# Own rows and projected rows turned by transposing DMAs in place of TensorE, in a two-layer, two-block graph network

## The chip, the cores and the metric
One core of one Trainium2 chip. The metric is the device time of one launch in microseconds (us), inputs and output in DRAM.

## The reference
x has 3125 nodes of 128 features; src and dst name 50,000 edges, sorted by dst. Two blocks follow each other; each adds a two-layer graph network of the normalised, rectified x to x.

```python
h = maximum(layernorm(x), 0)
# block 1: agg(h) = segment_sum(h[src], dst) * inv_deg
h1 = relu(concat([h, agg(h)]) @ W1 + b1)             # 128+128 -> 256
x  = x + log_softmax(concat([h1, agg(h1)]) @ W2 + b2)  # -> 128
h = maximum(layernorm(x), 0)
# block 2: mean(h) = segment_sum(h[src], dst) / max(deg, 1)
h3 = relu(mean(h)  @ W_l0.T + b_l0 + h  @ W_r0.T)    # -> 256
h4 = relu(mean(h3) @ W_l1.T + b_l1 + h3 @ W_r1.T)    # -> 256
out = x + relu(h4 @ W_lin1.T + b_lin1) @ W_lin2.T + b_lin2
```

## The kernel before
**Layout.** The nodes are cut into 25 tiles of 125 rows (P = 125) and seven chunks of columns: six full ones of 500 nodes (C, four tiles) and one of 125. Activations are kept in two ways: by rows, each node's values as an f16 high half and an f16 low half side by side (`hs_a`, `hs_b`, 125 partitions, per tile 2 x 128 columns), and turned, features on the partitions and nodes along the free side (`aggT`, `actT`, `zT`, `selfT`).

**Aggregation.** The edges are made into a dense matrix of edge counts, `adj`, in SBUF. `aggregate` (L1036) multiplies, for one chunk, every tile's high and low half by the 500 columns of `adj`: 50 matmuls per chunk and phase, accumulated in a bank of PSUM. `adj` is itself built by matmul: for each group DVE compares keys with a ramp (`group`, L493 for full chunks, L497 for the last), PE multiplies the one-hots (`count`, L990), and ACT copies the result out (L844). There are four buffers for one-hots, of which three go round, so DVE runs at most three groups ahead of PE.

**Phases.** Phase 1 aggregates the rows in `hs_a` and computes h1 and, because aggregation and projection commute, already projects: self = h1 times the own half of W2 (kept, stored to `self_d`), and z = h1 times the other half, scaled by a power of two, turned back to rows and written to `hs_b` as high and low halves. Phase 2 aggregates z, adds self, takes log_softmax, adds x (to `x1_d`), normalises, and writes the new rows to `hs_a`. Phase 3 aggregates them and makes h3; phase 4 aggregates h3 and ends with the two linear layers.

**Order within a chunk.** Each engine runs a program written out by hand; a step of chunk c also finishes chunk c-1. In phase 1 a step of PE (`step1`, L1112) is: own rows of chunk c-1 (`own1`, L1066: eight f16 matmuls by an identity, L1046, into bank 6); the first count and aggregate; six more; `hidden1` (eight f32 matmuls, L1053); six pieces; `second1` (eight more, for z and self); twelve pieces; `turn1` (L1086: four transposes of zT, L1090, into bank 3). Counts for chunk c+1 are woven between the aggregates of chunk c. The same step of DVE (L635): one group; `agg_out` (L615, scaling by the inverse degrees; it waits for their load); three groups; `low` of chunk c-2 (L626, low half of z); groups 4 to 18; `self_out` (L621); groups 19 to 24. ACT (L883): `h0_turned` (L856, bank 6 to aggT); `high` (L876); the evictions of the counts, with `relu` (L863) and `z_out` (L871) between. The first chunk (`first1`) has no predecessor; step 1 (`second=True`) also computes the bounds for the power-of-two scales and turns the weights.

Phases 2 to 4 share `staged` (L1176): chunk 0 is aggregated first, with the last parts of the phase before at set tiles (`lead`), then each step runs its `parts` at set tiles. Phase 3's parts are `own3` (L1250) at tile 0, `turn3` at 0, `hidden3` (L1254) at tile 8; ACT copies bank 3 to aggT (L957). At tiles 20 and 24 of chunk 0 PE waits for the last rows of the phase before (`source`).

**Queues.** All loads and stores of the layers are issued by SP, in one program and one queue. In phase 1 it stores the inverse degrees (L276), waits for them, loads those of chunk 0 (L291), and then per chunk waits for `p1_agg_out`, loads the next inverse degrees, waits for `p1_self` and stores self (L321); in step 0 it also stores the turned weights (L272), for which it waits. In phase 2 it loads inverse degrees, self and x, and stores x1 (L351). In phase 3 it loads inverse degrees and stores h3. A general path (`slow`) for graphs that do not fit the buffers is in the same program; a flag computed from the data picks one.

```python
def wait_past(eng, name, value):
    if not isinstance(value, int) or value > 0:
        eng.wait_ge(sem(name), value)
```

## Time and profile before

| | |
|---|---|
| median of 3 runs (lowest, highest) | 588.14 us (587.84, 588.85) |
| the profiled execution's own time | 587.56 us |
| its span, first to last instruction | 585.7 us |
| mean granted TensorE clock | 0.992 |
| PE busy | 544.2 us, 3078 matmuls |
| DVE, ACT, POOL busy | 225.0, 202.9, 24.7 us |
| own-row matmuls (L1046), all phases | 100, eight to a full chunk |
| DMA traffic | 29.47 MB, mean 50 GB/s |

Busy is the time in which an engine executes something; the span is 1.86 us shorter than the time. "Idle before, releaser" names what an engine waited for. The chain is the sequence of work that ended last, followed back from the end; its starts and durations follow the completion of each piece and so differ by some tenths from the timeline's. L numbers are lines of the kernel. DMA share is the mean busy share of 16 DMA engines. The phases lie at about 48 to 203 us (phase 1), 203 to 282 (phase 2), 282 to 380 (phase 3) and from there on (phase 4); building the first part of `adj` and normalising x fill the time before 48.

### The profile page before, as it was taken

The page shows a single profiled execution, that of the slowest core. Times are in us where ns is not written, and L with a number is a line of the kernel's source. Part 1 is how long each engine was busy: PE and PEld are TensorE (multiplying, and loading weights), DVE is VectorE, ACT ScalarE, POOL GpSimd, SP SyncE. Part 2 cuts the span into 40 slices and gives each one's busy share as a digit, 9 for nine tenths or more (in the row PEclk, how much of TensorE's full clock was granted, in tenths as well). Part 3 has the DMA queues.
Part 4 walks back from the last instruction along what each step waited for, and adds up shares of the span by engine and source line. Part 5 has one row for each costly group of instructions (what it writes and reads, how often), then busy time and mean ns, then how long its engine had stood idle before and what let it go on. Part 6 is the DMA issues. An engine that isn't in the chain of part 4 may idle for free.

```text
span 585.7 us, 9420 instructions
## 1 busy us (share of the span) xinstructions
PE 544.2 (93%) x3078; PEld 291.5 (50%) x3078; DVE 225.0 (38%) x500; ACT 202.9 (35%) x368; POOL 24.7 (4%) x36
## 2 busy tenths in 40 slices
PE   1367999999999999999999999999999999999996
PEld 0244655555554654445455555644545445454555
DVE  6899959577775217667411111110000001010001
ACT  1688858567664304455422222200000010100011
POOL 4410000000000000110100000000000000000000
PEclk9997999999999999999999999999999999999999
DMA  3800103010010124333121111232011212111011
GB/s 94 196 1 1 38 1 117 2 36 17 17 35 17 24 70 112 90 90 77 39 76 53 52 52 39 67 117 52 19 35 39 49 35 52 35 35 52 17 32 30
DMA packets 31372, 29.47 MB, mean 50 GB/s; under 512 B 4894, under 2 KB 30879, under 8 KB 31215
## 3 DMA queue, kind: packets, MB, share of 16 engines
q1 hardware_dynamic: 29622, 27.91, 17.6%
q10 hardware_dynamic: 1561, 0.84, 0.6%
q0 software_dynamic: 160, 0.33, 0.2%
q8 instruction: 18, 0.29, 0.2%
q14 instruction: 11, 0.09, 0.0%
HBM read 19.68 MB, written 9.39 MB: 50 GB/s over the span
## 4 chain that ended last, share of the span: by engine, by line
PE 87%; DVE 5%; ACT 3%; DMA 2%; issue 2%; POOL 1%; ACTq 0%; SPq 0%; DVEq 0%; POOLq 0%
PE ps L1036 54%; PE ps L1053 22%; PE ps L990 6%; PE ps L1308 2%; DVE hs_b L493 2%; PE ps L1046 1%; PE ps L1270 1%; DMA hs_b<-self_d 1%; DMA adj<-key_d,adj 1%; ACT adj L1490 1%; POOL adj L1375 1%; PE ps L1242 1%; DVE adj L1426 1%; DMA adj<-in_dst_dram 0%; ACT adj L844 0%
## 5 line engine op out<-in xcount | busy, mean ns | idle before, releaser
L1036 PE MATMUL ps<-adj,hs_b 125*128 (+2 forms) x1050 | 203.6, 351 | 0.0
L1036 PE MATMUL ps<-adj,hs_a 125*128 (+2 forms) x700 | 158.5, 353 | 0.0
L1036 PEld LDWEIGHTS ps<-adj,hs_b 125*128 125x128 f16 x1050 | 96.3, 97 | 103.9 <-issue 6.6
L493 DVE TENSOR_TENSOR hs_b<-iota,hs_b 128x1024 f16<-128x1024 f16 x150 | 95.4, 685 | 27.9 <-PE ps L990 26.9
L844 ACT ACTIVATE adj<-ps 125x500 f32 (+2 forms) x150 | 80.0, 544 | 22.8 <-PE ps L990 16.6
L990 PE MATMUL ps<-hs_b 128*128 128x125 f16 x625 | 68.5, 233 | 20.7 <-DVE hs_b L493 13.1
L990 PEld LDWEIGHTS ps<-hs_b 128*128 128x128 f16 x625 | 46.5, 103 | 65.7 <-DVE hs_b L493 34.4
L1036 PEld LDWEIGHTS ps<-adj,hs_a 125*128 125x128 f16 x700 | 58.5, 98 | 38.8 <-issue 5.4
L975 ACT ACTIVATE actT<-ps,col 128x500 f32<-128x500 f32 (+1 forms) x14 | 8.9, 633 | 148.0 <-PE ps L1053 148.0
L791 DVE TENSOR_TENSOR hs_a<-ps,hs_a 125x512 f32<-125x512 f32 (+1 forms) x7 | 4.4, 634 | 128.9 <-PE ps L1308 128.9
L1053 PE MATMUL ps<-aggT,wts 128*128 128x500 f32 (+1 forms) x112 | 44.6, 540 | 0.4 <-ACT aggT L957 0.4
L759 DVE TENSOR_TENSOR aggT<-ps,invc 128x500 f32<-128x500 f32 (+1 forms) x7 | 4.4, 622 | 64.9 <-PE ps L1036 61.6
L1053 PEld LDWEIGHTS ps<-aggT,wts 128*128 128x128 f32 x112 | 19.8, 190 | 18.8 <-issue 17.2
L782 DVE TENSOR_TENSOR aggT<-ps,invc 128x500 f32<-128x500 f32 (+1 forms) x14 | 8.7, 619 | 50.1 <-PE ps L1036 44.9
L1053 PE MATMUL ps<-wts,hs_a 128*128 128x500 f32 (+1 forms) x56 | 23.5, 541 | 0.6 <-DVE aggT L782 0.6
L1053 PE MATMUL ps<-aggT,hs_a 128*128 128x500 f32 (+1 forms) x56 | 23.3, 538 | 0.0
L1053 PE MATMUL ps<-actT,hs_a 128*128 128x500 f32 (+1 forms) x56 | 22.3, 541 | 0.5 <-ACT actT L975 0.5
L1053 PE MATMUL ps<-actT,wts 128*128 128x500 f32 (+1 forms) x56 | 22.3, 540 | 0.1
L979 ACT ACTIVATE aggT<-ps,col 128x500 f32<-128x500 f32 (+1 forms) x14 | 8.9, 633 | 35.2 <-PE ps L1053 35.1
L962 ACT ACTIVATE actT<-ps,col 128x500 f32<-128x500 f32 (+1 forms) x14 | 10.0, 723 | 30.4 <-PE ps L1053 30.4
L966 ACT ACTIVATE hs_b<-ps 125x512 f32 (+2 forms) x13 | 6.9, 578 | 36.6 <-PE ps L1270 36.6
L450 POOL TENSOR_TENSOR st<-st,col 125x4 f32<-125x4 f32 (+1 forms) x7 | 8.8, 1250 | 247.5 <-DVE st L259 247.5
(150 smaller groups left out, 356.4 us busy)
## 6 DMA issues: line engine op xcount, KB each, us to landing
invc<-inv_d SPq DMA_DIRECT2D x24, 250.0 KB, 3.3
h_d<-actT SPq DMA_DIRECT2D x6, 500.0 KB, 3.1
wts<-h_d SPq DMA_DIRECT2D x6, 500.0 KB, 4.0
self_d<-hs_b SPq DMA_DIRECT2D x6, 250.0 KB, 2.1
hs_b<-self_d SPq DMA_DIRECT2D x6, 250.0 KB, 3.5
hs_b<-in_x_dram SPq DMA_DIRECT2D x6, 250.0 KB
x_d<-hs_b SPq DMA_DIRECT2D x6, 250.0 KB
hs_a<-x_d SPq DMA_DIRECT2D x6, 250.0 KB
```

What stands on the lines that cost most here:

```text
L450: nc.gpsimd.tensor_tensor(st[0:P, 16:16 + nt], st[0:P, 12:12 + nt], mhalf[0:P, 0:nt], ALU.pow).then_inc(sem("p2_rstd"), 1)
L493: last = nc.vector.tensor_tensor(onehots[slot], iota2.unsqueeze(1).to_broadcast(shape), keys[:, ds(g * 4, 4), :].unsqueeze(2).to_broadcast ...
L782: nc.vector.tensor_tensor(aggT[:, h * C:h * C + n], bank(h, n), invc[:, 0:n], ALU.mult).then_inc(sem("p4_agg_out"), 1)
L844: nc.scalar.activation(columns(c, full, i * nd, nd), bank(k, nd * S, P).rearrange("p (d t) -> p t d", t=S), ACT.Copy).then_inc(sem("evicte ...
L962: nc.scalar.activation(actT[:, m * C:m * C + n], bank(4 + m, n), ACT.Relu, bias=b3s[:, m:m + 1], scale=s3[:, m:m + 1]).then_inc(sem("p3_re ...
L966: nc.scalar.activation(hs_write(hbz, c, full, 0, H)[:, t0:t1], tiles(bank(6 + k, (t1 - t0) * H, P), H), ACT.Copy).then_inc(sem("p3_high"), 1)
L975: nc.scalar.activation(actT[:, m * C:m * C + n], bank(4 + m, n), ACT.Relu, bias=bl1c[:, m:m + 1]).then_inc(sem("p4_relu"), 1)
L979: nc.scalar.activation(aggT[:, m * C:m * C + n], bank(6 + m, n), ACT.Relu, bias=bac[:, m:m + 1]).then_inc(sem("p4_relu2"), 1)
L990: last = nc.tensor.matmul(bank(i % 2 if b is None else b)[:, w * WD * S:(w + 1) * WD * S], onehots[slot][:, w // 2, :, w % 2], onehots[slo ...
L1036: last = nc.tensor.matmul(acc[:, 0:n], hs[:, ds(s * (2 * w) + part * w + h * 128, 128)], adj[0:P, ds(c * (S * C) + s * n, n)], start=(isin ...
L1053: last = nc.tensor.matmul(bank(b, n), wt, v, start=(k == 0), stop=(k == len(terms) - 1))
L1308: last = nc.tensor.matmul(bank(2, 4 * D, P)[:, t * D:(t + 1) * D], aggT[:, k * C + t * P:k * C + (t + 1) * P], bv[:, k, :], start=(k == 0) ...
```

## The change
For the six full chunks, own rows (phases 1 and 3) and z (phase 1) are no longer turned by PE.

- Rows in DRAM. In phase 1 SP waits for the low halves and stores all of `hs_a` to `hs_d1` in one DMA, before the load of inverse degrees of chunk 0. In phase 2 it stores each finished chunk of `hs_a` to `hs_d3`, one chunk late.
- Own rows. `turn_own` issues two transposing DMAs per chunk, one for the high and one for the low halves: 512 rows of 128 f16 values from DRAM into 128 partitions of 512 columns. DVE's `own_sum` adds the two into aggT behind `agg_out`. The next chunk's transposes are issued once the buffers are read.
- z. ACT writes the high half of z as f16 (`z16[0]`, in zT, tiles 128 columns apart), DVE the low half (`z_low`, behind `self_out`), and SP issues eight transposing DMAs of 128 x 128 per chunk, from zT into the rows of `hs_b`. ACT's next `z_out` waits until all eight have landed (`p1_zin`), PE's `second1` for the low half before, and phase 2 for the z of its tiles.
- The last chunk (125 nodes) and the slow path keep the old way. `own1` of chunk 6 waits for the low half of chunk 5's z. Some semaphores are merged; POOL zeroes zT at the start.

In the diff below the hunks of SP come first, then those of DVE (-620, -637), ACT (-867, -882) and PE (-1064, -1242).

```diff
+        PT = 128
+        z16 = [zT[:, :].bitcast(F16)[:, k * 4 * PT:(k + 1) * 4 * PT] for k in range(2)]
+        turned1 = [hs_b[:, (20 + 2 * k) * 2 * D:(22 + 2 * k) * 2 * D] for k in range(2)]
+        turned3 = z16
...
+            def turn_own(ph, c, hd, into):
+                for k in range(2):
+                    sp.dma_start_transpose(into[k], hd[ds(c * C, 512), k * D:(k + 1) * D]).then_inc(sem(f"p{ph}_hT"), 16)
             def spread(ph, hs, w, hd):
-                if slow:
+                if slow or ph == 1:
...
+            if not slow:
+                sp.wait_ge(sem("n_low"), S // PIECE)
             spread(1, ha, D, hs_d1)
             load_inv("p1_", 0, True)
+            if not slow:
+                sp.wait_ge(sem("rows"), 16)
+                turn_own(1, 0, hs_d1, turned1)
@@ -317,8 +332,17 @@ def step1(c, full, nxt):
                 if not slow and isinstance(c, int) and c == 0:
                     store_weights()
+                if not slow and nxt:
+                    sp.wait_ge(sem("p1_h0T"), c + 1)
+                    turn_own(1, c + 1, hs_d1, turned1)
                 sp.wait_ge(sem("p1_self"), c + 1)
                 sp.dma_start(self_d[:, ds(c * C, width(full))], selfT[:, 0:width(full)]).then_inc(sem("p1_self_out"), 16)
+                if not slow and full:
+                    sp.wait_ge(sem("p1_zlo"), c + 1)
+                    for t in range(4):
+                        for k in range(2):
+                            sp.dma_start_transpose(hs_b[:, ds(c * (4 * 2 * D) + (2 * t + k) * D, D)],
+                                                   z16[k][:, t * PT:(t + 1) * PT]).then_inc(sem("p1_zin"), 16)
@@ -350,17 +374,30 @@ def step2(c, full, nxt):
+                if not slow and not (isinstance(c, int) and c == 0):
+                    sp.wait_ge(sem("p2_low"), c)
+                    sp.dma_start(hs_d3[ds((c - 1) * C, C), :].rearrange("(t p) f -> p t f", p=P),
+                                 ha[:, ds((c - 1) * (4 * 2 * D), 4 * 2 * D)].rearrange("p (t f) -> p t f", f=2 * D)).then_inc(
+                        sem("p2_rows"), 16)
...
             load_inv("p3_", 0, True)
+            if not slow:
+                sp.wait_ge(sem("p2_rows"), 16 * NFULL)
+                turn_own(3, 0, hs_d3, turned3)
+                sp.dma_start(hs_d3[NFULL * C:N, :], ha[:, NFULL * 4 * 2 * D:S * 2 * D]).then_inc(sem("p2_rows"), 16)
+                sp.wait_ge(sem("p2_rows"), 16 * NCH)
...
+                if not slow and nxt:
+                    sp.wait_ge(sem("p3_ownT"), c + 1)
+                    turn_own(3, c + 1, hs_d3, turned3)
@@ -620,9 +657,22 @@
+            def own_sum(ph, c, parts):
+                dve.wait_ge(sem(f"p{ph}_hT"), 32 * c + 32)
+                wait_past(dve, "p1_h1" if ph == 1 else "p3_h3", 2 * c)
+                nc.vector.tensor_tensor(aggT[:, C:2 * C], parts[0][:, 0:C], parts[1][:, 0:C], ALU.add).then_inc(
+                    sem("p1_h0T" if ph == 1 else "p3_ownT"), 1)
+            def z_low(c):
+                dve.wait_ge(sem("p1_zT"), c + 1)
+                by_tile = lambda v: v.rearrange("p (t n) -> p t n", n=PT)[:, :, 0:P]
+                nc.vector.scalar_tensor_tensor(by_tile(z16[1]), bank(6, C).rearrange("p (t n) -> p t n", n=P), zs, by_tile(z16[0]),
+                                               ALU.mult, ALU.subtract).then_inc(sem("p1_zlo"), 1)
@@ -637,6 +687,7 @@ def step1(c, full, nxt, second=False):
                 agg_out(c - 1, True)
+                own_sum(1, c - 1, turned1)
                 if nxt is not None:
                     build_b(c + 1, nxt)
...
-                else:
-                    low(c - 2, True)
-                    if nxt is not None:
-                        build_c(c + 1, nxt, 0, 5)
+                elif nxt is not None:
+                    build_c(c + 1, nxt, 0, 5)
                 self_out(c - 1, True)
+                z_low(c - 1)
@@ -867,12 +918,21 @@ def z_out(c, full):
+                if full and not slow:
+                    wait_past(act, "p1_zin", 128 * c)
+                    nc.scalar.activation(z16[0].rearrange("p (t n) -> p t n", n=PT)[:, :, 0:P],
+                                         bank(6, n).rearrange("p (t n) -> p t n", n=P), ACT.Identity, scale=zs).then_inc(
+                        sem("p1_zT"), 1)
+                    return
@@ -882,9 +942,6 @@ def step1(c, full, nxt, second=False):
-                h0_turned(c - 1, True)
-                if not second:
-                    high(c - 2, True)
@@ -1064,7 +1122,10 @@ def own1(c, full):
+                    pe.wait_ge(sem("p1_zlo"), NFULL)
                 own(ha, D, 0, 6, c, full).then_inc(sem("p1_own"), 1)
...
-                own1(c - 1, True)
...
-                if second:
-                    pe.wait_ge(sem("wt"), 5)
-                turn1(c - 1, True)
@@ -1242,13 +1307,15 @@
-                   [(0, own1, NFULL), (6, hidden1, NFULL), (12, second1, NFULL), (17, turn1, NFULL)], (NFULL - 1, NFULL, NCH))
+                   [(0, own1, NFULL), (6, hidden1, NFULL), (12, second1, NFULL), (17, turn1, NFULL)],
+                   (("p1_zin", 128 * (NFULL - 1)), ("p1_zin", 128 * NFULL), ("p1_low", 1)))
...
-            staged(3, [(lambda c: bank(acc3(c, slow)), ha, D, 0)], [(0, own3, 1), (8, hidden3, 1), (0, turn3, 2)],
+            staged(3, [(lambda c: bank(acc3(c, slow)), ha, D, 0)], ([(0, own3, 1)] if slow else []) + [(8, hidden3, 1), (0, turn3, 2)],
```

## Rows read from the trace of the kernel before
**Rows 1.** The page: busy time (share, instructions), and the chain by engine.
```profile
PE 544.2 (93%) x3078; PEld 291.5 (50%) x3078; DVE 225.0 (38%) x500; ACT 202.9 (35%) x368; POOL 24.7 (4%) x36
...
PE 87%; DVE 5%; ACT 3%; DMA 2%; issue 2%; POOL 1%; ACTq 0%; SPq 0%; DVEq 0%; POOLq 0%
```
**Rows 2.** Busy by stage (us of the stretch, each engine, clock, DMA share, GB/s).
```profile
146.80:172.00 25.20, 24.84 (x181) 13.76 (x179) 17.48 (x29) 17.36 (x30) 0.00 (x0) 1.00 0.07 20
...
316.80:363.10 46.30, 46.30 (x232) 23.60 (x230) 6.15 (x10) 9.30 (x15) 0.00 (x0) 1.00 0.14 50
```
**Rows 3.** Timeline at phase 1's start (start us, us, engine, line, operation).
```profile
57.23 0.82 DVE L527 TENSOR_TENSOR hs_a<-hs_b,hs_a 125x640 f16<-125x640 f32 x1
...
61.98 7.35 SPq L291 DMA_DIRECT2D invc<-inv_d  x2
...
68.30 0.68 DVE L615 TENSOR_TENSOR aggT<-ps,invc 128x500 f32<-128x500 f32 x1 [1.02 <-PE ps L1036]
...
68.89 1.89 DVE L493 TENSOR_TENSOR hs_b<-iota,hs_b 128x1024 f16<-128x1024 f16 x3
...
70.46 0.39 PE L990 MATMUL ps<-hs_b 128*128 128x125 f16 x4
```
**Rows 4.** Busy, clock and DMA over chosen stretches (columns as in rows 2).
```profile
24.00:28.00 4.00, 1.45 (x12) 0.92 (x10) 3.93 (x22) 4.00 (x9) 1.35 (x1) 1.00 1.11 357
...
45.00:51.00 6.00, 3.72 (x25) 2.25 (x23) 5.26 (x11) 4.51 (x7) 0.00 (x0) 0.50 0.01 3
...
235.00:240.00 5.00, 5.00 (x25) 2.28 (x24) 3.58 (x13) 1.04 (x4) 1.38 (x1) 1.00 0.33 95
280.00:283.50 3.50, 3.50 (x18) 1.57 (x17) 1.90 (x10) 1.01 (x4) 1.38 (x1) 1.00 0.29 74
420.00:427.50 7.50, 7.50 (x37) 3.48 (x36) 0.32 (x2) 0.00 (x0) 0.00 (x0) 1.00 0.29 68
```
**Rows 5.** DMA issues of SP (count, KB each, median us to landing).
```profile
self_d<-hs_b SPq DMA_DIRECT2D x6, 250.0 KB, 2.1
hs_b<-self_d SPq DMA_DIRECT2D x6, 250.0 KB, 3.5
```
**Rows 6.** Timeline of a middle step of phase 1.
```profile
146.59 0.68 DVE L615 TENSOR_TENSOR aggT<-ps,invc 128x500 f32<-128x500 f32 x1 [0.84 <-PE ps L1036]
...
166.06 0.73 DVE L621 TENSOR_SCALAR hs_b<-ps,col 128x500 f32<-128x500 f32 x1
...
166.71 3.69 DVE L493 TENSOR_TENSOR hs_b<-iota,hs_b 128x1024 f16<-128x1024 f16 x6
...
167.52 0.40 PE L990 MATMUL ps<-hs_b 128*128 128x125 f16 x4
```
**Rows 7.** The chain in the same step (start us, us, engine, line).
```profile
145.97 0.42 PE ps L1036 x2
...
152.87 3.37 PE ps L1053 x8
```
**Rows 8.** Timeline where phase 1 ends and phase 2 begins.
```profile
201.91 0.74 DVE L621 TENSOR_SCALAR hs_b<-ps,col 128x500 f32<-128x500 f32 x1 [6.98 <-PE ps L1053]
...
210.28 0.37 ACT L871 ACTIVATE zT<-ps,col 128x125 f32<-128x125 f32 x1 [2.61 <-PE ps L1053]
...
212.63 0.28 PE L1090 MATMUL ps<-identf,zT 128*125 128x128 f32 x1
```
**Rows 9.** Timeline at the end of phase 2 and in phase 3.
```profile
279.22 9.08 SPq L351 DMA_DIRECT2D x_d<-hs_b  x2
...
293.99 0.68 DVE L759 TENSOR_TENSOR aggT<-ps,invc 128x500 f32<-128x500 f32 x1 [3.26 <-DMA invc<-inv_d]
...
296.35 3.52 PE L1053 MATMUL ps<-aggT,wts 128*128 128x500 f32 x8
...
365.39 1.94 PE L1053 MATMUL ps<-aggT,wts 128*128 128x500 f32 x4 [0.41 <-ACT aggT L957]
```
**Rows 10.** The chain in phase 3: own rows of one chunk.
```profile
347.42 0.44 PE ps L1046 x8
```

More of the change, by code:

```diff
@@ L869, in z_out @@
                 act.wait_ge(sem("scale3"), 2)
-                wait_past(act, "p1_turned", c)
+                if full and not slow:
+                    wait_past(act, "p1_zin", 128 * c)
[3 more added lines that the diff above has]
+                    return
+                if slow:
+                    wait_past(act, "p1_turned", c)
+                else:
+                    act.wait_ge(sem("p1_zin"), 128 * NFULL)
                 nc.scalar.activation(zT[:, 0:n], bank(6, n), ACT.Identity, scale=zs).then_inc(sem("p1_zT"), 1)
@@ L954, in step3 @@
                 nt = n // P
-                act.wait_ge(sem("p3_own"), c + 1)
-                wait_past(act, "p3_h3", 2 * c)
-                nc.scalar.activation(aggT[:, C:C + n], bank(3, n), ACT.Copy).then_inc(sem("p3_ownT"), 1)
+                by_dma = full and not slow
+                if not by_dma:
+                    act.wait_ge(sem("p3_own"), c + 1 if slow else 1)
+                    wait_past(act, "p3_h3", 2 * c)
+                    nc.scalar.activation(aggT[:, C:C + n], bank(3, n), ACT.Copy).then_inc(sem("p3_ownT"), 1)
                 wait_past(act, "p3_turned", 2 * c)
@@ L1081, in second1 @@
                 pe.wait_ge(sem("p1_relu"), 2 * c + 2)
+                if not slow:
+                    wait_past(pe, "p1_zlo", c)
                 dense(6, n, [(w2v[:, 2 + m, :], actT[:, m * C:m * C + n]) for m in range(2)]).then_inc(sem("p1_zm"), 1)
@@ L1087, in turn1 @@
                 pe.wait_ge(sem("p1_zT"), c + 1)
-                wait_past(pe, "p1_low", c)
+                if slow:
+                    wait_past(pe, "p1_low", c)
                 for t in range(width(full) // P):
```

53 lines of the change are left out of this document (30 added, 23 removed).

## The prediction

> **What bounds the kernel now.** I read the page's busy times and its chain first: TensorE (PE) is busy 93% of the span and makes 87% of the chain, with VectorE (DVE) 5% behind it [rows 1]. That speaks for any change that takes work off PE. So the next view is by stage, to see whether PE is alone there. In a middle step of phase 3 PE is busy all 46.3 us of 46.3 while DVE is busy 6.15 [rows 2]: work taken off PE there comes back in full. In a middle step of phase 1 PE is busy 24.84 of 25.2, but DVE 17.48, and DVE builds the one-hot matrices that PE's counts read, from a ring that lets it run only three groups ahead. The timeline of one such step [rows 6] shows how close it is: the group built after the self output starts at 166.71 and takes 0.69 us, so it is done at 167.40, and PE counts it at 167.52. DVE has 0.1 us in hand there. Phase 1 is bound by both engines in turn.
>
> Then the start of phase 1, because the change puts a transfer there [rows 3]. The last low half of the rows is written at 57.23 to 58.05; the first load of inverse degrees is issued at 61.98 (behind the inverse degrees' own store); DVE scales the aggregate of chunk 0 at 68.30 and builds the next groups from 68.89; PE counts the second of them at 70.46. Nothing on DVE waits for a DMA there now.
>
> **The sum is made against the profiled execution:** 587.56 us, of which the span is 585.7; the median of the three runs is 588.14, so 0.58 is added at the end. A measurement of this kernel can tell about 0.2% (1.2 us) from no change.
>
> **1. The store of all rows (phase 1), new, and what waits for it.** SP issues it once the low halves are done and the inverse degrees have landed, so at 61.98, ahead of the first load of inverse degrees, and then waits for it before it issues the two transposes of chunk 0. DVE waits for that load in its scaling of chunk 0, and for the transposes in the new sum right behind, which stands ahead of the three builds of 68.89. So the path is store, transposes, sum, build, count, and PE has one piece of work left in the meantime.
> Size: 3125 rows of 512 bytes, 1.6 MB. Rate: the nearest rows are the stores and loads of 512-byte rows over the same 125 partitions, 256 kB each. One alone (280 to 283.5) moved 74 GB/s at a DMA share of 0.29, a load and a store together 95 GB/s at 0.33, and a store and a load behind each other 68 GB/s at 0.29 [rows 4]. A share of 0.3 of 16 engines is five engines. The loads of x over 112 partitions moved 357 GB/s with all engines. The new store has 125 partitions, so I take 85 GB/s, between 68 and 95: 1.6 MB take 18.8 us (16.8 to 23.5). With 0.8 us to the first bytes (estimated from the store issued at 279.22 [rows 9] and its bytes from 280 on) and 0.5 to the receipt, the rows are in DRAM at 82.1. The load of inverse degrees is queued behind it on those engines and lands about then as well.
> No row shows a transposing DMA. Between 2.1 us (the 250 KB store of the self rows) and two loads of 3.5 us one after the other, 7.0 [rows 5], I take one 3.5, since the two move 256 kB together, as that load does, and 0.7 for two issues: 86.3. The sum of two f16 halves costs DVE 0.60 (from one start to the next, as its scaling of the same width, 68.30 to 68.89): 86.9. A build 0.69: PE counts at 87.7 what it counted at 70.46. That is **+17.2**.
> The clock: with PE waiting some 16 us, the granted clock should fall. From 45 to 51 us, after a stretch with PE half idle, it was 0.50 (1.2 GHz) [rows 4]. Three or four slow pieces at twice 0.65 us cost up to 2; DVE's work on the weight bounds made PE wait about 1.2 there anyway. I take **+0.7** (0 to 2). The queue for chunk 1's transposes then has the store of the weights (1152 KB) ahead of it, but is issued some microseconds before the next scaling, so 0 (0 to 2). Bounds of part 1: 13 (95 GB/s, 2.1 us, no clock) and 26 (68 GB/s, 7.0 us, 2 for the clock).
>
> **2. The other steps of phase 1.** PE loses eight small matmuls (own rows) and four transposes per full chunk, 0.44 us each. But the order on DVE behind the last aggregate of a chunk is now scaling 0.60, sum 0.60, build 0.69, so the second count comes 0.2 (146.39 to 146.59) + 1.89 = 2.1 us after it, while PE has only 0.65 us of its own to do. Six more pieces at 0.655 bring the dense matmuls to 6.1 us after the aggregate; now it is 6.5 (the chain has 146.39 to 152.87) [rows 7]. Gain 0.35 instead of 0.88, in three steps: -1.05. The low half of z moves behind the self output, exactly where DVE has 0.1 us in hand: 0.6 us more there makes PE wait 0.5, in four steps: +2.0. In step 5 the groups are a quarter of the size and DVE has room: 0. In step 6 PE's 0.88 makes way for the wait on DVE's sum (about 0.5): -0.4; the last transposes are gone, but the own rows of chunk 6 now wait for the low half of z: -0.2. ACT loses an eviction and a copy per chunk, which bound only for a few tenths; counted in the 0.35. Sum **+0.35** (-2 to +3).
>
> **3. Eight transposes of z per chunk.** ACT may write the next z only when they have landed, a period of 25 us later, less in the last two steps, which have little or nothing to build. For chunk 5, the self output ends at 202.65 and z's low half at 203.2 [rows 8]; eight issues of 0.45 (an estimate, from SP's 0.34 and 0.43 for plain ones) and 3.5 to the last landing give 210.7. z of chunk 6 is written at 210.28 now and turned by PE at 212.63, so 1.9 us of slack hide it; PE reads the rows at its tile 20, about 213.9. I take **0** (0 to 15, see the second rival). What hides it is that the eight overlap in the queue.
> The Trainium skill, page "VectorE: DVE Perf Modes", section "The three transpose paths", has 1309 ns for one 128x128 transpose by DMA; eight in a row by that would land at about 214.5 and cost some 2.5 us at PE's turn of z, and the whole would be 607.4 rather than 604.9. Its page "Advanced Engine Details and Errata", section "X-Bar Transpose (TRN2)", says they are as fast as regular DMAs, which would leave the term at 0. No row here shows either.
>
> **4. Phase 2** gains a 256 kB store per chunk on SP, behind the store of x1, some 3.4 us of five engines, next to a load and a store that take as long. The loads that DVE needs next are issued most of a chunk ahead: 0 (0 to 2).
>
> **5. Start of phase 3.** The store of chunk 5's rows is issued behind the last store of x1 (288.3) and is done 3.4 us after its first bytes, landing near 293.5 [rows 9]. DVE has already waited 3.26 us for the load of inverse degrees when it scales at 293.99. Behind the rows the two transposes land at 293.5 + 0.7 + 3.5 = 297.7 less what overlaps, say 297; the sum ends at 297.6 and PE's dense matmuls, at 296.35 now, start at 297.65: **+1.3**, own rows of chunk 0 included (bounds -0.4 and +5).
> **6. The rest of phase 3:** eight matmuls, 0.44 us of the chain [rows 10], five more times, and in the last of them ACT's eviction of 0.6, for which PE waits 0.41 [rows 9], turns into DVE's: -2.2 - 0.4 = **-2.6**. DVE's sum (0.6) is hidden: PE has 3.4 us of tiles between.
> POOL's new memset of zT lies in the first microseconds, beside loads: 0. Phase 4 is untouched.
>
> Sum: 587.56 + 17.2 + 0.7 + 0.35 + 0 + 0 + 1.3 - 2.6 = 604.5; in terms of the median 605.1. I put **605**.
>
> **Rivals.** *A, it ends faster or level: the store of the rows goes out on all 16 engines.* At 357 GB/s it takes 4.5 us: rows at 67.8, transposes at 72.0 (70.6 if they land in 2.1), sum and build at 73.3, count 3.0 us late (1.6). With part 5's store fast too (-0.4) the whole is 587.56 + 3.0 + 0.35 - 0.4 - 2.6 + 0.58 = 588.5; with the short landing and DVE's place for z not binding, 585. The point from which it decides: the wait at the first sum below about 2 us. For it: the loads over 112 partitions. Against it: every transfer over 125 partitions shows 0.3 of the engines. Chance 0.19, of it 0.11 faster.
> *B, the transposes do not overlap.* At 2.1 us each, eight of chunk 4 take 17 us where I estimate 10 to 11 between its z and the next (+6.5), those of chunk 5 hold back z of chunk 6 by 8, in all about +15: 620. At 3 us ten fill 30 us of a 25 us period: beyond 635. For it: nothing shows them overlap, and ACT waits for all eight. Against it: other DMAs of this queue overlap (5 us for a load and a store). Chance 0.14.
> *C, only part of the wait of part 1 appears* (the store faster than 95 GB/s, or the transposes short): 590 to 598. Chance 0.07. That the change does nothing where it claims to is excluded by the code: both paths are switched by the flag that this data passes.
>
> **Numbers.** Forecast with its own bounds, 598 to 614: 0.60; B 0.14, A 0.19, C 0.07. Range 588 to 624: it leaves out A's lower part (0.12) and B's upper (0.07). Faster by over 0.2%: 0.11; within: 0.06; slower: 0.83.
>
> **What would show it.** Right: PE idle for some 16 us near 70 to 87 with a granted clock near 0.5 afterwards; DVE's scaling of chunk 0 waiting on the load of inverse degrees until about 82, its sum on a transpose; DMA share 0.3 over that stretch; waits of counts for builds behind the self output; phase 3 steps shorter by 0.44. Wrong: a share near 1 for the store, or ACT's z waiting on DMA, step after step.

## Result and the profile after

The changed kernel takes 611.22 us (median of four runs, 609.72 to 611.61) against 588.50 for the kernel before: a ratio of 1.038, interval 1.0353 to 1.0405. It is slower by 22.7 us; the forecast was 605.0 with a range of 588 to 624. The profiled execution took 611.43 us with a span of 609.6, 23.9 more than before's 585.7. One execution of a later kernel (the rows in five pieces) took 610.55 us at a mean granted clock of 0.952, where its three others have 0.988 to 0.991; it is left out of that kernel's median.

The page of the changed kernel, busy time (share, instructions) and the chain by engine; it answers to [rows 1]:

```profile
PE 542.5 (89%) x2958; PEld 283.2 (46%) x2958; DVE 232.2 (38%) x512; ACT 194.5 (32%) x350; POOL 25.3 (4%) x37
...
PE 67%; issue 11%; DMA 9%; DVE 6%; SPq 3%; ACT 3%; POOL 1%; DVEq 0%; ACTq 0%; POOLq 0%
```

120 matmuls fewer have taken only 1.7 us off PE's busy time (some of the others run at a lower clock and take longer), and the span has grown by 23.9: the loss is time in which PE stands, 25.6 us more than before. Of the chain PE has 67% in place of 87%; DMA has 9%, and SP's own queue (SPq) 3%, which was 0 before.

Where the span went is read by laying the first dense matmuls of each chunk side by side (start in us; in phase 2 the first transpose of a chunk):

| point | before | after | later by | new in this step |
|---|---|---|---|---|
| last low half of the rows | 57.23 | 58.02 | 0.8 | 0.8 |
| second count behind chunk 0 | 70.46 | 84.86 | 14.4 | 13.6 |
| dense, chunk 0 | 76.11 | 91.53 | 15.4 | 1.0 |
| dense, chunk 1 | 102.02 | 119.08 | 17.1 | 1.6 |
| dense, chunk 5 | 193.92 | 213.07 | 19.2 | 2.1 |
| phase 2, chunk 0 | 219.60 | 241.36 | 21.8 | 2.6 |
| phase 2, chunk 6 | 282.17 | 303.94 | 21.8 | 0.0 |
| phase 3, dense, chunk 0 | 296.35 | 320.64 | 24.3 | 2.5 |
| phase 3, dense, chunk 1 | 306.15 | 331.96 | 25.8 | 1.5 |
| phase 3, dense, chunk 5 | 365.39 | 389.57 | 24.2 | -1.6 |
| end of the span | 585.7 | 609.6 | 23.9 | -0.3 |

**Start of phase 1.** The chain of the changed kernel (start us, us, what), which answers to [rows 3]:

```profile
62.67 16.89 DMA hs_d<-hs_a
...
79.58 1.25 SPq L302
80.83 0.05 issue
80.88 2.63 DMA hs_b<-hs_d
83.50 0.02 issue
83.53 0.68 DVE aggT L663
```

The timeline of the same stretch, with what each instruction waited for in brackets:

```profile
80.20 0.68 DVE L652 TENSOR_TENSOR aggT<-ps,invc 128x500 f32<-128x500 f32 x1 [12.13 <-DMA invc<-inv_d]
81.02 0.99 PE L1094 MATMUL ps<-adj,hs_a 125*128 125x500 f16 x2 [10.54 <-DVE aggT L652]
...
83.53 0.68 DVE L663 TENSOR_TENSOR aggT<-hs_b 128x500 f32<-128x500 f16 x1 [2.65 <-DMA hs_b<-hs_d]
84.12 1.89 DVE L530 TENSOR_TENSOR hs_b<-iota,hs_b 128x1024 f16<-128x1024 f16 x3
...
84.86 0.60 PE L1048 MATMUL ps<-hs_b 128*128 128x125 f16 x4 [2.85 <-DVE hs_b L530]
```

Stretches of it (us, PE busy, clock, DMA share, GB/s):

```profile
64.00:76.00 12.00, 6.49 (x60) 0.85 0.36 107
76.00:84.00 8.00, 0.99 (x2) 0.50 0.45 111
84.00:88.00 4.00, 3.14 (x17) 0.50 0.18 42
88.00:92.00 4.00, 3.82 (x25) 0.82 0.01 4
```

The store of the rows holds everything: 16.89 us at a DMA share of 0.36 and 107 to 111 GB/s. The load of inverse degrees lands behind it at 80.2, the transposes at 83.5, and PE finds its clock at half (1.2 GHz) until past 88. The Trainium skill, page "DMA: Bandwidth & Descriptors", section "Why a DMA increments its semaphore by 16 and not by 1", says that such a transfer runs on the largest number up to 16 that divides the slowest dimension of both sides; for 125 that is 5 of 16. That would be a share of 0.31; the trace roughly agrees, with 0.36 while the load of inverse degrees is queued beside the store.

**The projected rows (z).** The queue of SP and the instructions that wait for it, where phase 1 ends (compare [rows 8]):

```profile
208.00 10.62 SPq L344 DMA_TRANSPOSE hs_b<-zT  x8
...
222.48 10.03 SPq L344 DMA_TRANSPOSE hs_b<-zT  x8
...
219.88 0.68 ACT L923 ACTIVATE zT<-ps,col 128x500 f16<-128x500 f32 x1 [2.53 <-DMA hs_b<-zT]
233.76 0.37 ACT L931 ACTIVATE zT<-ps,col 128x125 f32<-128x125 f32 x1 [7.06 <-DMA hs_b<-zT]
...
234.18 0.38 PE L1154 MATMUL ps<-identf,zT 128*125 128x128 f32 x1 [2.35 <-ACT zT L931]
```

A transposing DMA keeps SP's queue for about 1.25 us (10.03 to 10.86 for eight, 2.54 for the first two), where most plain ones take 0.28 to 0.58. (Plain ones can be held up as well: the load of inverse degrees behind the big store keeps the queue for 13.46 us, the stores of rows in phase 2 for up to 1.71.) The eight of chunk 5 are issued from 222.48 to 232.51, ACT can write the next z only at 233.76, and PE waits 2.35 for it.

**Start of phase 3**, the timeline (compare [rows 9]):

```profile
310.11 0.34 SPq L379 DMA_DIRECT2D hs_d<-hs_a  x1
...
315.95 2.44 SPq L302 DMA_TRANSPOSE zT<-hs_d  x2
...
319.91 0.68 DVE L663 TENSOR_TENSOR aggT<-zT 128x500 f32<-128x500 f16 x1 [2.11 <-DMA zT<-hs_d]
320.64 5.32 PE L1111 MATMUL ps<-aggT,wts 128*128 128x500 f32 x8 [2.80 <-DVE aggT L663]
```

A stretch of it, columns as in [rows 2]:

```profile
320.00:328.00 8.00, 7.36 (x21) 3.50 (x22) 0.84 (x2) 1.53 (x2) 0.00 (x0) 0.79 0.35 67
```

PE waits 2.80 us for the own rows' sum, and the eight dense matmuls behind it take 5.32 us where they took 3.5, at a granted clock of 0.79 over that stretch. From 304 to 320 the clock was 1.00.

### The profile page after: what moved, and what is told of

The parts are those of the page before. It is cut to its first block, busy times and chain, and to the rows that moved or that the text cites. A ratio compares the mean times of both kernels' runs of the same rounds, so it can differ in the third digit from the quotient of the medians.

```text
span 609.6 us, 9253 instructions
## 1 busy us (share of the span) xinstructions
PE 542.5 (89%) x2958; PEld 283.2 (46%) x2958; DVE 232.2 (38%) x512; ACT 194.5 (32%) x350; POOL 25.3 (4%) x37
## 4 chain that ended last, share of the span: by engine, by line
PE 67%; issue 11%; DMA 9%; DVE 6%; SPq 3%; ACT 3%; POOL 1%; DVEq 0%; ACTq 0%; POOLq 0%
PE ps L1094 38%; PE ps L1111 21%; PE ps L1048 5%; DMA hs_d<-hs_a 4%; PE ps L1375 2%; DVE hs_b L530 2%; SPq L344 1%; DMA hs_b<-in_x_dram 1%; DMA hs_b<-hs_d 1%; SPq L302 1%; PE ps L1337 1%; DMA invc<-inv_d 1%; ACT adj L1558 1%; DMA adj<-in_dst_dram 1%; DMA adj<-key_d,adj 1%
## 5 line engine op out<-in xcount | busy, mean ns | idle before, releaser
L1094 PE MATMUL ps<-adj,hs_a 125*128 (+2 forms) x700 | 160.3, 356 | 12.7 <-DVE aggT L652 12.4
L1048 PE MATMUL ps<-hs_b 128*128 128x125 f16 x625 | 69.3, 235 | 28.2 <-DVE hs_b L530 19.2
L1111 PE MATMUL ps<-aggT,wts 128*128 128x500 f32 (+1 forms) x112 | 46.3, 558 | 2.8 <-DVE aggT L663 2.8
```

The source lines that it names most:

```text
L1048: last = nc.tensor.matmul(bank(i % 2 if b is None else b)[:, w * WD * S:(w + 1) * WD * S], onehots[slot][:, w // 2, :, w % 2], onehots[slo ...
L1094: last = nc.tensor.matmul(acc[:, 0:n], hs[:, ds(s * (2 * w) + part * w + h * 128, 128)], adj[0:P, ds(c * (S * C) + s * n, n)], start=(isin ...
L1111: last = nc.tensor.matmul(bank(b, n), wt, v, start=(k == 0), stop=(k == len(terms) - 1))
```

## The experiments

All are compared with the kernel before, timed on the same chip beside them (588.56 to 588.84 us).

**The three parts alone.** Each kernel is the kernel before with one part of the diff.

Phase 3's own rows only (phase 1 as before):

```diff
+                if not slow and nxt:
+                    sp.wait_ge(sem("p3_ownT"), c + 1)
+                    turn_own(3, c + 1, hs_d3, turned3)
...
+                if full and not slow:
+                    own_sum(3, c, turned3)
...
-            staged(3, [(lambda c: bank(acc3(c, slow)), ha, D, 0)], [(0, own3, 1), (8, hidden3, 1), (0, turn3, 2)],
+            staged(3, [(lambda c: bank(acc3(c, slow)), ha, D, 0)], ([(0, own3, 1)] if slow else []) + [(8, hidden3, 1), (0, turn3, 2)],
```

> Only the own rows of phase 3 go by DMA; phase 1 is as before. Theory (each part costs where its first use waits): the step of chunk 0 in phase 3 starts 2.4 us late behind the store of chunk 5's rows and two transposes, the clock that falls in that wait costs another 1.9, and five steps give back 2.2: 590.5 (589 to 592). Rival (the transposes pay once they have a chunk's time to land, and the loss in the changed kernel is all phase 1's): 586.0, below the kernel before by the 2.6 us that the prediction gave phase 3.

Measured: 590.38 us, ratio 1.003 (1.0016 to 1.0044). The number is the theory's, the way to it only in part. The trace has phase 3's first dense matmuls 2.1 us later against phase 2's than before (16.31 us behind its last transpose in place of 14.18), and 2.2 us come back by the end. But the clock does not fall in the wait, so the 1.9 us put on it do not come:

```profile
301.12 3.62 PE L1085 MATMUL ps<-aggT,wts 128*128 128x500 f32 x8 [2.41 <-DVE aggT L649]
```

What makes up for it is a start of the program 2.3 us late (first dense matmuls of phase 1 at 78.37, before 76.11), which no theory named. So phase 3's part about pays for itself in this trace, and the hit is in part luck. The rival's 586.0 does not come here; its idea, that the transposes pay once they have time to land, returns in a later run.

The projected rows only:

```diff
+                    for t in range(4):
+                        for k in range(2):
+                            sp.dma_start_transpose(hs_b[:, ds(c * (4 * 2 * D) + (2 * t + k) * D, D)],
+                                                   z16[k][:, t * PT:(t + 1) * PT]).then_inc(sem("p1_zin"), 16)
...
-                turn1(c - 1, True)
```

> Only z goes by DMA (eight transposes a chunk); own rows are turned by PE in phases 1 and 3. Theory: each transpose occupies the issuing queue for 1.24 us, so that eight take 10 us; hidden under a full step, not at the end of phase 1, where z of the last chunk waits for them: +2.6 and +0.6 there, about -0.3 in each of four steps: 590.5 (589 to 593). Rival (it is the DVE instruction for z's low half behind the self output that costs, in every step): each step of phase 1 longer by 0.5 than before, and the end as before: 591, but told apart by the step times in the trace.

Measured: 594.57 us, ratio 1.0098 (1.0081 to 1.0116). Missed by 4: the kernel takes 6.0 us longer. In the profiled execution the span is 7.1 us longer. 2.5 of them are there by the first dense matmuls of phase 1 (78.58), ahead of any z; 0.7 come up to chunk 5's; 4.4 between those and the first transpose of phase 2 (30.03 us in place of 25.68). The rival's 0.5 us in every step is not there either: from dense to dense the three middle steps take 0.14 to 0.20 longer, and only the last one, to chunk 5, 0.57. The timeline has the same waits as the full change, and the stretch behind them (columns as in [rows 2]) a clock of 0.61:

```profile
206.50 10.79 SPq L331 DMA_TRANSPOSE hs_b<-zT  x8
218.50 0.37 ACT L896 ACTIVATE zT<-ps,col 128x125 f32<-128x125 f32 x1 [7.78 <-DMA hs_b<-zT]
...
218.92 0.57 PE L1113 MATMUL ps<-identf,zT 128*125 128x128 f32 x1 [3.06 <-ACT zT L896]
```

```profile
218.00:222.00 4.00, 3.08 (x8) 1.36 (x9) 0.29 (x1) 0.65 (x2) 0.00 (x0) 0.61 0.39 110
```

The own rows of phase 1 only:

```diff
+                    turn_own(1, c + 1, hs_d1, turned1)
...
+                own_sum(1, c - 1, turned1)
...
-                h0_turned(c - 1, True)
...
-                own1(c - 1, True)
```

> Only the own rows of phase 1 go by DMA. Theory (the store of all rows, on five engines, and what is queued behind it hold DVE up at chunk 0): 13.6 us at the start, 1.0 for the clock, 1.6 at chunk 1, whose transposes are issued behind the wait for the weights' store; steps after that as before: 604.5 (602 to 607). Rival (several small waits add up, and the start is only one of them): below 600.

Measured: 605.69 us, ratio 1.0297 (1.0274 to 1.0319), so 17.1 us of the 22.7, within the expected range. In this kernel DVE's scaling of chunk 0 waits 12.35 us for the load of inverse degrees, as in the change (12.13). The three parts sum to 1.8 + 6.0 + 17.1 = 24.9, a little over the whole. Part of that is the start of the program: the last low half of the rows is 2.2, 2.5 and 1.7 us late in the three kernels (59.45, 59.68, 58.90) and 0.8 in the whole change, so the same kind of delay is counted three times.

**The rate of the store.** The whole change, the store of phase 1 cut at partition 112:

```diff
-                if slow or ph == 1:
+                if slow:
...
+                elif ph == 1:
+                    for a, b in WHOLE16:
+                        sp.dma_start(hd.rearrange("(t p) f -> p t f", p=P)[a:b],
+                                     hs.rearrange("p (t f) -> p t f", f=2 * w)[a:b]).then_inc(sem("rows"), 16)
```

> The changed kernel with the store of all rows cut into partitions 0 to 111 and 112 to 124. Theory (125 partitions put it on five engines, DMA share 0.36 and 109 GB/s): the first part goes out on all engines at about 350 GB/s, the rows are there 10 us sooner, the first sum and the builds with them, and the clock falls for less time: 611.2 - 10.5 - 0.5 = 600 (598 to 603). Rival (the load of inverse degrees and the two transposes bound it, not the store): over 608.

Measured: 602.54 us, ratio 1.0226 (1.02 to 1.0252), 8.7 us less than with one store and within the expected range. A stretch of the store, in all columns:

```profile
64.00:68.00 4.00, 4.00 (x38) 2.40 (x36) 3.98 (x7) 3.67 (x8) 0.00 (x0) 1.00 1.02 265
```

The share is 1.02 and the rate 265 GB/s where they were 0.36 and 107. The rows are in DRAM at 71.36, 8.7 us after the first issue at 62.67, in place of 16.89. The first dense matmuls come at 83.18 in place of 91.53: 8.4 us of the 15.4 are back. So the narrow store was about half of the loss of the start. The next run tests whether the rest is that the store begins only when everything is computed.

**The store's place.** The rows go out in five pieces as their low halves become ready, and chunk 1's transposes are issued ahead of the weights' store:

```diff
+                for j in range(S // PIECE):
+                    sp.wait_ge(sem("n_low"), j + 1)
+                    for a, b in WHOLE16:
+                        sp.dma_start(hs_d1[PIECE * j * P:PIECE * (j + 1) * P, :].rearrange("(t p) f -> p t f", p=P)[a:b],
+                                     ha.rearrange("p (t f) -> p t f", f=2 * D)[a:b, PIECE * j:PIECE * (j + 1)]).then_inc(
+                            sem("rows"), 16)
...
-                    store_weights()
                     turn_own(1, c + 1, hs_d1, turned1)
+                    store_weights()
```

> The changed kernel, with two orders altered on the sync engine's queue and nothing else: the rows of phase 1 are stored in five pieces of five tiles, each as soon as its low halves are ready and each in a 112-partition and a 13-partition part, and chunk 1's transposes are issued ahead of the weights' store. Theory: the loss at the start of phase 1 is the wait for that store and what hangs on it (13.6 us at the first counts of chunk 2, some 0.6 us of slow clock behind it, 1.6 us at chunk 1). Then the first dense block starts near 77.5 us in place of 91.7 and the kernel takes 611.2 - 14.2 - 1.6 = 595.4 us (593 to 598). Rival: the rows are only one of the things that are late (the inverse degrees or the transposes themselves keep the vector engine), and more than a third of the loss stays: over 600.

Measured: 599.32 us (596.64 to 599.67), ratio 1.0182 (1.0161 to 1.0203), 11.9 under the change; the profiled execution took 596.64, 14.8 under. The profiled time lies in the expected range, the median is 3.9 us above the expected value and outside the range. The mechanism is there: the sum on DVE waits for nothing now.

```profile
70.26 0.68 DVE L658 TENSOR_TENSOR aggT<-ps,invc 128x500 f32<-128x500 f32 x1 [1.02 <-PE ps L1100]
70.85 0.67 DVE L669 TENSOR_TENSOR aggT<-hs_b 128x500 f32<-128x500 f16 x1
71.44 1.89 DVE L536 TENSOR_TENSOR hs_b<-iota,hs_b 128x1024 f16<-128x1024 f16 x3
```

The first dense matmul comes at 78.66 (91.53 in the change), 12.9 us earlier of the 14.2 looked for, and chunk 1's at 104.74 (119.08), 14.3 of 15.8. So nearly all of the start's loss was the store, its rate and its place. Why the other runs lie up to 3 us above the profiled one no trace shows.

**Phase 3's start.** Added to that: chunk 0 of phase 3 is transposed ahead of chunk 5's loads in phase 2, and GpSimd clears z's buffer later. The second run has phase 3's part alone with the same early transposes and no clearing at all.

```diff
             def step2(c, full, nxt):
+                if not slow and full and nxt is False:
+                    sp.wait_ge(sem("p2_rows"), 16 * (NFULL - 2))
+                    turn_own(3, 0, hs_d3, turned3)
```

> The run before, and two more: the transposes for chunk 0 of phase 3 are issued in phase 2, ahead of its chunk 5, and GpSimd's memset of the buffer of projected rows comes after its share of the layer norm in place of before the identity matrices. Theory: the first removes the 2.4 us by which the first dense block of phase 3 was late and the 2.0 us that its lower clock cost, the second 0.7 us at the program's start: 595.4 - 5.1 = 590.3 us (588.5 to 592). What is then left over the kernel before is the projected rows' share and the waits at the steps' starts. Rival: the load of the inverse degrees ends as late as the transposes did, so that phase 3 gives back under 1 us: 593.5 to 595.

> The kernel before with phase 3's part of the change alone, its chunk 0 transposed during phase 2, and no memset of the buffer. Theory: against the same part with the late transposes and the memset (590.4 us) it gains 2.3 us at the first dense block of phase 3, and 0.7 us or more at the program's start: 587.0 us (585.5 to 588.0), so faster than the kernel before by some 1.5 us, because the ten own-row products per step of phase 3 are gone from TensorE and nothing has taken their place. Rival: the stores of rows in phase 2, and not the transposes, are what phase 3 waits for: 588.5 to 590.

Measured: 593.68 us, ratio 1.008 (1.0063 to 1.0096), and for phase 3 alone 588.62, ratio 1.0009 (0.9995 to 1.0023). Both missed, by 3.4 and 1.6 us, and both lie in the range of their rival. Against the run before it (599.32) the first is 5.6 us lower, though, where 5.1 was looked for. The start of phase 3, which both rivals name, is not what is late: its first dense matmuls come 13.73 and 13.74 us behind phase 2's last transpose, before 14.18 and in the change 16.70. The queue of SP in the second shows what is:

```profile
278.53 2.76 SPq L302 DMA_TRANSPOSE zT<-hs_d  x2
281.34 0.58 SPq L296 DMA_DIRECT2D invc<-inv_d  x1
281.97 0.42 SPq L343 DMA_DIRECT2D hs_b<-self_d  x1
```

The two transposes stand ahead of chunk 6's loads, and from chunk 5's first transpose on PE to chunk 6's phase 2 takes 10.07 us (10.30 in the first of the two) where it took 8.59. I had moved the wait from one queue position to another. Leaving out GpSimd's clearing of the buffer did not bring the first dense matmul of phase 1 back either (77.68 in this kernel, before 76.11), so that guess is not borne out.

Then the own rows of both phases with both early starts, while PE goes on turning z (the parts of the diff for the own rows, the pieces and the early transposes as above, none for z):

> Own rows of phases 1 and 3 by transposing DMAs, both with their first chunk early (rows of phase 1 stored in pieces, chunk 1 ahead of the weights' store), projected rows turned by TensorE as before, no memset. Theory: own rows in phase 1 alone took 605.7 us; less 15.8 us of start and chunk 1 that leaves 589.9, less 1.5 us of phase 3 and 0.7 us of memset 587.7 us (586 to 590): no better than phase 3 alone, because the middle steps of phase 1 gain nothing (from the first to the sixth dense block they took 1.4 us longer). Rival: with the start repaired, the products taken from TensorE show as a gain in phase 1 too, 0.4 us a step: under 585.5.

Measured: 591.44 us (588.99 to 592.28), ratio 1.0046 (1.0032 to 1.0061): no better than phase 3 alone, and worse than it by 2.8 us where 0.7 was expected; the median lies above the expected range, the profiled 588.99 in it. From the dense matmuls of chunk 1 to those of chunk 5 phase 1 takes 92.14 us (104.77 to 196.91), before 91.90 (102.02 to 193.92), though eight matmuls a chunk are gone from PE. And the repaired start is still not free: DVE scales chunk 0 at 68.31, as before (68.30), but the sum now stands ahead of its three builds, PE waits 1.98 us for one of them in place of 1.16, the granted clock is 0.70 from 76 to 80 us where it was 1.00, and the first dense matmuls come at 78.29 in place of 76.11.

**The transposes behind the loads.**

```diff
                              tiles(x1b[:, 0:width(full) // P * D], D)).then_inc(sem("p2_x1_out"), 16)
+                if not slow and full and nxt is False:
+                    sp.wait_ge(sem("p2_rows"), 16 * (NFULL - 2))
+                    turn_own(3, 0, hs_d3, turned3)
```

> Phase 3's part alone again, with its first two transposes issued behind the loads and the first store of phase 2's chunk 5 in place of ahead of them. In the run before they held the sync engine's queue for 2.76 us while chunk 6's loads stood behind them, and phase 2 ended 1.0 us later. Theory: that 1.0 us comes back: 588.6 - 1.0 = 587.6 us (586.8 to 588.4), 1 us under the kernel before. Rival: phase 2's end is late for another reason and nothing comes back: 588.3 to 589.3.

Measured: 586.11 us (585.83 to 586.87), ratio 0.9963 (0.9949 to 0.9976). **This beats the kernel before**, by 0.4%, clear of the noise. Chunk 5 to chunk 6 takes 8.59 again:

```profile
275.14 0.42 SPq L343 DMA_DIRECT2D hs_b<-self_d  x1
277.58 0.30 SPq L346 DMA_DIRECT2D hs_b<-in_x_dram  x1
279.76 0.31 SPq L361 DMA_DIRECT2D x_d<-hs_b  x1
280.11 3.03 SPq L302 DMA_TRANSPOSE zT<-hs_d  x2
```

It came 1.5 us lower than expected. Between the two profiled executions 1.1 us is the first dense matmul of phase 1 (76.60 against 77.68), which no edit between the two touches; that much of the gain is not the edit's.

**The end of z.** The whole change with these early starts, and a buffer of its own for z of chunk 6:

```diff
-                    act.wait_ge(sem("p1_zin"), 128 * NFULL)
-                nc.scalar.activation(zT[:, 0:n], bank(6, n), ACT.Identity, scale=zs).then_inc(sem("p1_zT"), 1)
+                nc.scalar.activation((zT if slow else z6)[:, 0:n], bank(6, n), ACT.Identity, scale=zs).then_inc(sem("p1_zT"), 1)
```

> The whole change with both early starts (593.7 us), the two transposes of phase 3 behind chunk 5's loads as in the run above, and the projected rows of the part chunk 6, which TensorE turns, in a buffer of their own, so that ScalarE need not wait until all eight transposes of chunk 5 have read theirs. Theory: the eight transposes at 1.24 us of the sync engine's queue each are what holds the end of phase 1 and the start of phase 2; of their cost the 2.4 to 3.1 us that TensorE stood before chunk 6's turn comes back, and 1.0 us at phase 2's end: 590.3 us (589 to 591.5). Rival: phase 2's first aggregation waits for the same transposes (chunk 5's rows are its own source), so that the stall only moves by some us: 592 to 593.7.

Measured: 594.88 us (592.05 to 597.48), ratio 1.0102 (1.0067 to 1.0138), no better than the run with the early starts alone (593.68) and above even the rival's range. What the rival names is what happened: the wait has only moved, to PE's aggregation over chunk 5's rows and to a load of inverse degrees that stands in SP's queue behind the eight transposes.

```profile
220.78 5.25 PE L1102 MATMUL ps<-adj,hs_b 125*128 125x500 f16 x24 [1.76 <-DMA hs_b<-zT]
...
226.29 0.74 DVE L759 SCALAR_TENSOR_TENSOR aggT<-ps,col,invc 128x500 f32<-128x500 f32 x1 [7.90 <-DMA invc<-inv_d]
```

The clock then falls to 0.70 from 230 to 234 us, and phase 2's second chunk comes 12.79 us behind its first, before 11.11.

**Phase 1's steps.** Two accumulator banks in turn from chunk 2 on, and the sum behind the three builds (the loops over the middle chunks are also written out):

```diff
+            return 2 if slow or c < 2 else 2 + (c + 1) % 2
...
-                own_sum(1, c - 1, turned1)
                 build_b(c + 1, nxt)
+                own_sum(1, c - 1, turned1)
```

> The run above, and in phase 1 the chunks from the second on take two accumulator banks in turn (the one that turned the projected rows is free) and the own rows' sum comes behind the next three groups' build on the vector engine. Theory: the middle steps gained nothing from the products taken off TensorE because the work removed had covered the eviction of the single bank (0.25 us a step) and the vector engine's groups (0.40 us a step); both come back in five steps: 590.3 - 3.0 = 587.3 us (586 to 588.5). Rival: the steps go at the pace at which the vector engine and ScalarE build, and another wait of the same length follows: within 1 us of the run above.

Measured: 592.88 us (592.53 to 593.18), ratio 1.0076 (1.0061 to 1.0092). The median is 2.0 under the run before it, between theory and rival, but the two intervals overlap: no gain is shown by the times. From chunk 1's dense matmuls to chunk 5's it takes 92.51 us (106.20 to 198.71) against 94.06: 1.55 back, 0.4 a step, from the banks and the new order together. PE no longer waits for the accumulator, but it does for what is built:

```profile
151.74 0.39 PE L1059 MATMUL ps<-hs_b 128*128 128x125 f16 x4 [0.49 <-ACT adj L906]
...
155.07 0.40 PE L1059 MATMUL ps<-hs_b 128*128 128x125 f16 x4 [0.25 <-DVE hs_b L541]
```

The step before them gives the same time away. From chunk 0's dense matmuls to chunk 1's it takes 27.87 us in place of 26.18, because the granted clock is down when the eight dense matmuls of chunk 0 come (5.65 us for them, 3.67 in the run before); the matmul and a stretch, columns as in the first stretches above:

```profile
78.33 5.65 PE L1122 MATMUL ps<-aggT,wts 128*128 128x500 f32 x8
...
76.00:80.00 4.00, 4.00 (x14) 0.50 0.02 4
```

Chunk 5's dense matmuls so come at 198.71, in the run before at 198.88. What the profiled execution has gained (3.2 us) lies behind them, at the start of phase 2, where PE waits 0.49 us for chunk 5's rows in place of 1.76 and the clock stays at 1.00.

**Phase 3's steps.** The best version, with two accumulator banks in phase 3 (and the loops over its middle chunks written out):

```diff
-            return 1 if isinstance(c, int) and c == 1 and not slow else 2
+            return 1 if not slow and c % 2 == 1 else 2
```

> Phase 3's part alone with its first transposes behind chunk 5's loads (586.1 us), and the chunks of phase 3 take two accumulator banks in turn. Theory: of the 0.6 us that eight own-row products took a step only 0.24 came off, because TensorE now comes back from the transposes before the vector engine has read the single accumulator (it starts again 0.26 us after the last transpose). With two banks that goes in four steps: 586.1 - 1.0 = 585.1 us (584.6 to 585.8). Rival: the 0.26 us is TensorE's own, and nothing changes: 585.8 to 586.6.

Measured: 585.66 us (584.57 to 586.24), ratio 0.9944 (0.993 to 0.9958), 3.2 us under the kernel before. Against the run with one bank (ratio 0.9963) the intervals overlap, so the times alone do not show the second bank's gain; the steps do: from dense to dense 14.80 us (307.58 to 322.38) in place of 15.03 (306.41 to 321.44) and 15.28 before. First the run with one bank, then that with two:

```profile
331.99 1.04 PE L1304 MATMUL ps<-identf,actT 128*125 128x128 f32 x8
332.28 0.68 DVE L789 TENSOR_TENSOR aggT<-ps,invc 128x500 f32<-128x500 f32 x1 [12.53 <-PE ps L1069]
...
333.10 3.55 PE L1069 MATMUL ps<-adj,hs_a 125*128 x16
```

```profile
332.92 1.04 PE L1308 MATMUL ps<-identf,actT 128*125 128x128 f32 x8
333.79 3.54 PE L1069 MATMUL ps<-adj,hs_a 125*128 125x500 f16 x16
```

PE goes on 1.11 us after the start of the transposes with one bank (332.96 is when DVE has read it), 0.87 with two. Writing out the loops is not what does it, or not most of it: the last step was written out before too, and there the same gap is 1.03 with one bank and 0.88 with two. The profiled execution is no shorter than the one with one bank because the program's start is 1.5 us later (dense of chunk 0 at 78.10 against 76.60).

## Why the prediction was right, and which terms were off

The direction and the main mechanism were right: of 23.9 us, 15.4 are there by the first dense matmuls of phase 1, and the runs with the store on all engines and with the store in pieces take 8.7 and 11.9 us off (the second 14.8 in the profiled execution). That the forecast is only 6.2 us low is in part luck. By the trace the sum was 6.9 us short (16.95 against 23.9): six smaller terms were 10.2 us too low together, and the main one 3.3 too high.

**Part 1, +17.2 and +0.7.** Measured 13.6 to the second count and 1.0 more to the dense matmuls, 14.6 for 17.9. The store moved at 107 to 111 GB/s, above my upper bound of 95, so 16.89 us in place of 20; the two transposes took 3.9 from issue to landing against 4.2 assumed. Chunk 1's transposes behind the weights' store, put at 0 (0 to 2), cost 1.6: SP stood until 106.74 waiting for the turned weights, the issue began at 107.11 and took 4.52 us, with the weights' store moving beside it, and DVE's sum waited 1.37 us for them and PE 1.87 for the build behind it. I had counted on an issue "some microseconds before the next scaling".

**Part 2, +0.35.** Measured 2.1 in four steps. That z's low half stands where DVE has no room was right (PE waits 0.50 there), but its +2.0 was too much: with z alone the four steps take 1.1 us longer. With phase 1's own rows alone they take 0.3 longer, so what failed is the gain of -1.05 set against it. By the waits, the own-row matmuls had covered the time in which DVE reads the single accumulator bank and ACT evicts: with them gone PE waits 0.49, 0.25 and 0.41 at a step's start. Two banks and the sum behind the builds took 0.4 a step off; the builds of DVE and ACT then bound. Why both parts together cost 2.1 and not 1.4 is not shown. Work taken off PE in these steps gave nothing.

**Part 3, 0.** Measured 2.6 in the change, 4.4 at the same place with z alone. The step that failed is "eight issues of 0.45": an issue is 1.25 us. (The working has slips that change nothing: 203.2, 3.6 and 3.5 make 210.3, and the 604.9 named there is 604.5 or 605.1 in the sum.) The landings do overlap, so rival B (2.1 us each, one behind the other, +15) was too dark. The Trainium skill, page "VectorE: DVE Perf Modes", section "The three transpose paths", gives 1309 ns for one 128x128 transpose, and the +2.5 at PE's turn of z that was worked out from it is near what came: PE waits 2.35 there in the change, 3.06 with z alone. Its page "Advanced Engine Details and Errata", section "X-Bar Transpose (TRN2)", calls them as fast as regular DMAs; in the queue of SP, where 1.25 us stands against 0.28 to 0.58 for most plain ones, this trace does not agree.

**Part 4, 0**: held; phase 2 takes what it took, to 0.01 us.

**Part 5, +1.3.** Measured 2.5, and 1.5 more by chunk 1. The rows' store landed 5.8 us after its issue, not 5.2, the load of inverse degrees was itself later (4.62 us of waiting in place of 3.26), and the lower clock behind the wait had no term. With the transposes issued in time and behind the loads, all of it came back: phase 3's first dense matmuls come 14.07 us behind phase 2's last transpose, before 14.18.

**Part 6, -2.6.** Measured -1.6 from chunk 1 to chunk 5 and -0.3 behind it. The last of these steps gave 0.90 us, as forecast (0.44 and 0.41). In the middle ones 0.24 came of the 0.44 that the chain had shown, because the rest had covered DVE's reading of the bank; the run with two banks, with 0.24 more, shows it. The sentence that failed is "work taken off PE there comes back in full", read from PE being busy all of 46.3 us (which are three steps, not one: a step is 15.28).

**GpSimd's memset, 0**: the last low half is 0.8 later. It is not shown that the memset does this: the three kernels with phase 3's part and without the memset are late there too (57.73, 58.80 and 59.22 against 57.23), while the one with the own rows of both phases, also without it, has 57.23. Part of the difference is the clock. It is at half when phase 1 begins in the kernel before and in the others, a pair of aggregating matmuls then takes 0.83 us in place of 0.42, and it returns at different times. From 52 to 54 us, first the kernel before, then the last run (us, PE busy, clock, DMA share, GB/s):

```profile
52.00:54.00 2.00, 2.00 (x20) 1.00 0.00 0
```

```profile
52.00:54.00 2.00, 2.00 (x11) 0.50 0.00 0
```

Why it returns later in one kernel than in another is open. (In the first run of phase 3's part without the memset the record has 1.00 there although the matmuls take as long as at half.)

Rival A's engine share did not come (0.36), and rival C's range neither.

## What to carry to other kernels

Work taken off the busiest engine pays only where nothing else is due at that moment, even where that engine is busy all the time: look for what the removed work was covering (an accumulator being read, an eviction) before its time is counted as gain. A transposing DMA occupied its queue here for over a microsecond, so its place among that queue's loads decides, and a transfer that feeds it belongs where its data become ready, cut so that all engines share it. Here only phase 3's part was worth keeping: issued early and behind the loads, with a second bank, it is 3.2 us under the kernel before, while the whole change with repaired starts, a buffer of its own for the last z and a second bank in phase 1 stays 4.3 above it. Last, some 2 us of these differences are the program's start, which moves from kernel to kernel: compare stretches of the trace before a time of that size is put down to an edit.

## What the hardware showed that was not expected

- 1.25 us of SP's queue per transposing DMA, the same for 128x128 inside SBUF (10.03 us for eight) as for 512x128 from DRAM (2.43 to 2.54 for two). With other transfers under way it was at times longer (12.31 for eight, 4.52 for two).
- A share of 0.36 of the DMA engines and 107 GB/s for rows over 125 partitions against 1.02 and 265 GB/s when cut at 112 (350 had been looked for).
- A wait of 2.80 us before phase 3's first dense matmuls was followed by eight of them in 5.32 us; with phase 3's part alone a wait of 2.41 us was followed by the same eight in 3.62. PE was fully busy for some 12 us before either. So one of two nearly equal waits cost 1.7 us of clock and the other nothing; why is open.
